# Deformable convolution, second layer: four gathered taps in even tiles, three in odd ones, and column positions loaded over the partitions instead of spread by matmuls

## The reference, cut to what matters

```python
def _L1_conv_ref(x, w_p, b_p, w_m, b_m, w_conv):
    offset = _conv2d(x, w_p, b_p, padding=1)                   # 18 maps: 9 rows, 9 columns
    m = jax.nn.sigmoid(_conv2d(x, w_m, b_m, padding=1))        # 9 weights
    p = offset + p_0[None] + p_n[None, :, None, None]          # place of every tap
    ...
    x_off = g_lt * gather(q_lt_x, q_lt_y) + g_rb * gather(q_rb_x, q_rb_y) \
          + g_lb * gather(q_lt_x, q_rb_y) + g_rt * gather(q_rb_x, q_lt_y)
    x_off = x_off * m                                          # 9 taps of 32 channels
    return _conv2d(x_off, w_conv, None, stride=KS, padding=0)
...
x = x + _L0_conv_ref(_gn(x), ...)
x = x + _L1_conv_ref(_gn(x), ...)
```

## Time and profile before

| | before |
|---|---|
| three timed runs | 558.33, 562.84, 563.54 us; median 562.84 |
| profiled execution, its own time | 557.18 us |
| span of that execution | 555.1 us |
| TensorE busy | 492.3 us, 89% of the span, 4214 matmuls |
| VectorE busy | 422.8 us, 76%, 941 instructions |
| ScalarE busy | 155.5 us, 28% |
| GpSimd busy | 261.6 us, 47% |
| DMA | 48.10 MB, mean 87 GB/s |

### The profile page before, as it was taken

One profiled execution on the slowest core, in us unless ns is written; L12 is line 12 of the kernel. 1 busy time (PEld: TensorE's weight loads), 2 busy tenths in 40 slices (PEclk: granted clock), 3 DMA queues, 4 the chain that ended last, 5 costly groups with the idle time before them and its releaser, 6 DMA issues.

```text
span 555.1 us, 11479 instructions
## 1 busy us (share of the span) xinstructions
PE 492.3 (89%) x4214; PEld 286.5 (52%) x4214; DVE 422.8 (76%) x941; ACT 155.5 (28%) x292; POOL 261.6 (47%) x272
## 2 busy tenths in 40 slices
PE   3687879988937799999999999999999999999994
PEld 3345445646626435454555555555545555465553
DVE  2455385779846498887978879888888888899892
ACT  3321120211035522323324233232232332332211
POOL 2177455547100177454544545555545454555520
PEclk9857798989986999999999999999999999999998
DMA  4899479577303871122121229111111111111100
GB/s 110 251 227 228 119 179 185 115 132 139 73 4 93 242 171 53 52 59 56 54 57 52 74 60 114 43 35 44 39 39 44 39 44 34 46 37 44 44 21 14
DMA packets 39879, 48.10 MB, mean 87 GB/s; under 512 B 15742, under 2 KB 31906, under 8 KB 39824
## 3 DMA queue, kind: packets, MB, share of 16 engines
q1 hardware_dynamic: 31464, 30.20, 24.9%
q0 software_dynamic: 8192, 16.79, 12.1%
q10 hardware_dynamic: 168, 0.34, 0.2%
HBM read 30.62 MB, written 8.72 MB: 71 GB/s over the span
## 4 chain that ended last, share of the span: by engine, by line
PE 73%; DVE 11%; DMA 5%; SPq 5%; issue 3%; ACT 2%; POOL 0%; DVEq 0%; ACTq 0%
PE ps_later L1166 12%; PE ps_pair L1166 10%; PE ps_raw L1147 8%; PE ps_x L1179 8%; PE ps_x L1183 5%; PE ps_x L1191 5%; PE ps_raw L976 5%; DVE vlast L1602 3%; PE ps_o L1207 3%; DMA xn<-xq 3%; PE ps_o L989 3%; SPq L475 2%; PE ps_pair L1041 2%; PE ps_x L1041 2%; DMA shared<-positions 2%
## 5 line engine op out<-in xcount | busy, mean ns | idle before, releaser
L611 POOL DMA_INDIRECT got<-table,idx x256 | 254.4, 994 | 218.2 <-DVE prod L1803 112.5
L1786 DVE TENSOR_TENSOR samples<-shared,vprod 128x800 f32<-128x800 f32 x48 | 47.1, 985 | 15.9 <-PE ps_x L1041 10.8
L1179 PEld LDWEIGHTS ps_x<-early,vprod 128*128 128x128 f32 x384 | 43.2, 144 | 30.5 <-issue 28.3
L1602 DVE TENSOR_TENSOR vprod<-ps_pair,rhat 128x704 f32<-128x704 f32 x64 | 56.6, 885 | 2.0 <-PE ps_pair L1166 1.7
L1602 DVE TENSOR_TENSOR vprod<-ps_later,rhat 128x704 f32<-128x704 f32 x64 | 56.6, 884 | 0.6 <-PE ps_later L1166 0.4
L1147 PE MATMUL ps_raw<-conv_out,later 128*128 128x512 f32 x96 | 53.9, 643 | 1.4 <-ACT shared L830 1.4
L1179 PE MATMUL ps_x<-early,vprod 128*128 128x128 f32 x384 | 54.8, 279 | 0.0
L1612 DVE TENSOR_TENSOR vprod<-vprod 128x640 f32<-128x640 f32 x64 | 52.4, 819 | 0.3
L1602 DVE TENSOR_TENSOR vlast<-ps_pair,rhat 128x704 f32<-128x704 f32 x32 | 28.5, 891 | 27.0 <-PE ps_pair L1166 26.7
L1166 PE MATMUL ps_later<-columns_of,shared 64*64 64x352 f32 x384 | 38.8, 474 | 4.2 <-DVE vlast L1602 3.7
L1166 PE MATMUL ps_later<-columns_of 64*64 64x352 f32 x384 | 38.9, 475 | 4.1 <-DVE vlast L1602 4.0
(11 more groups left out here) (215 smaller groups left out, 711.7 us busy)
## 6 DMA issues: line engine op xcount, KB each, us to landing
shared<-positions SPq DMA_DIRECT2D x24, 440.0 KB, 10.4
xn<-xq SPq DMA_DIRECT2D x52, 132.0 KB, 3.9
got<-table,idx POOLq DMA_INDIRECT x256, 8.0
table<-trow SPq DMA_DIRECT2D x9, 234.0 KB
table<-trow SPq DMA_DIRECT2D x2, 1024.0 KB, 5.1
out<-ysumT SPq DMA_DIRECT2D x64, 16.0 KB, 1.5
columns_of<-table SPq DMA_DIRECT2D x2, 512.0 KB, 9.4
table<-trow SPq DMA_DIRECT2D x1, 936.0 KB
```

What stands on the lines that cost most here:

```text
L611: pool.indirect_dma_start(into[t][:, s * P:(s + 1) * P], None, tab, bass.IndirectOffsetOnAxis(ap=idx[:, slot, k:k + 1], axis=0),).then_inc ...
L1179: nc.tensor.matmul(bank[:, P:2 * P], vprod[:, t % 2, r, :], idn[:], start=(r == 0), stop=(r == HALF - 1), is_transpose=True)
L1602: nc.vector.tensor_tensor(dst, ps_dense[pair_number(0, t, pair) % 2][:].rearrange("p (d n) -> p d n", d=2)[:, :, 0:WROWS * C].rearrange("p ...
L1786: nc.vector.tensor_tensor(wprod[t % 2].rearrange("p (y x c) -> p y x c", y=SIDE, c=C), window[n // TT % NWIN][:, :, 2 * t * C:(2 * t + SID ...
```

## The change

Even tiles now gather four taps and odd tiles three. An even tile so has five dense taps: two pairs, and tap 8 alone. Tap 8 of tiles 0 and 2 share one pair, made with tile 0, so a group has 11 pairs instead of 12, and tile 2 has only two. Tap 8 of both tiles goes into `vlast`, the third pair of odd tiles into a new `vtail`; three additions instead of four; an even tile turns two blocks of it instead of four. The gathers rise from 12 to 14 a group.

The spreads are left in place for groups 0 to 2 only (in two or three smaller matmuls, since even and odd tiles now take other taps). For groups 3 to 15 one matmul, `fold_parts`, folds the four parts of `conv_out` and picks out six rows of column positions (33 rows in `ps_raw`), and ScalarE copies them to `folded` with even tiles in the first half and odd ones in the second (`copy_folded`). SP writes the six rows to DRAM (`send_places`), and in a later group six DMAs read them back so that 64 partitions each hold the same row (`load_places`, 704 KB a group; the source steps by 0 over the partitions). ScalarE then takes the absolute value in place, with the partition's own column as a bias, where it took it from PSUM before. `turn_folded` transposes the 27 folded rows instead of `turn_parts`. The convolution moves from t = 2 to t = 1, the fold stands at t = 2 behind the outputs. `later` grows from 1,092 to 1,879 columns.

```diff
-GT = 3
-DT = 9 - GT
+GT_OF = (4, 3)
+GT = max(GT_OF)
+DENSE = min(GT_OF)
+DT = 9 - DENSE
-PAIRS = 3 * TT
+PAIRS = 3 * TT - 1
+SPREAD_GROUPS = 3
-LATER = dict(fold_proj=P, conv_w1=4 * 32, grid1=27, grid2=27, w4=9 * C, steps1=WROWS, spread=SPREADS * P, wd0=C, wd=C, wlast=C,
+LATER = dict(fold_proj=P, conv_w1=4 * 32, grid1=TT * 27, rows1=NG * TT * GT, grid2=27, w4=9 * C, steps1=WROWS, spread=2 * SPREADS * P, wd0=C, wd4=C, wd3=C, wlast=C, fold1=27 + DT, away=1,
...
         def pairs_of(t):
-            return range(3)
+            return range(2 if t == 2 else 3)
...
+            def send_places(n):
+                sp.wait_ge(fold_sb, n - SPREAD_GROUPS + 1)
+                if n >= SPREAD_GROUPS + 2:
+                    sp.wait_ge(chat_come, 96 * (n - 1 - SPREAD_GROUPS))
+                sp.dma_start(places_of[n % 2], folded[27:27 + DT, :]).then_inc(places_out, 16)
+            def load_places(n):
+                sp.wait_ge(places_out, 16 * (n - SPREAD_GROUPS + 1))
+                sp.wait_ge(v_mm, 4 * PAIRS * (n - 1))
+                half, at = GPIX // 2, n % 2 * DT * GPIX
+                for h in range(2):
+                    to = chat[n % 2][W * h:W * (h + 1)]
+                    sp.dma_start(to[:, 0:2, 0:half], bass.AP(places_of.tensor, at + (1 + h) * GPIX, [
+                        [0, W], [2 * GPIX, 2], [1, half]])).then_inc(chat_come, 16)
+                    sp.dma_start(to[:, :, half:GPIX], bass.AP(places_of.tensor, at + h * GPIX + half, [
+                        [0, W], [2 * GPIX, SPREADS], [1, half]])).then_inc(chat_come, 16)
+                    sp.dma_start(to[:, 2, 0:P], bass.AP(places_of.tensor, at + (DT - 1) * GPIX + h * P, [
+                        [0, W], [1, P]])).then_inc(chat_come, 16)
...
+            for g in range(NG):
+                if SPREAD_GROUPS <= g + 1 < NG:
+                    load_places(g + 1)
+                for c in ROWS_IN.get(g, []):
                     sp.wait_ge(tab_copied, NT + PT + c + 1)
                     send_rows(table[1][1], range(c, c + 1), tab_out["11"])
...
+                if g + 3 < NG:
+                    send_places(g + 3)
+                if g:
+                    store((g - 1) // GB, (g - 1) % GB, (g - 1) % 2)
+                if PT - 1 in ROWS_IN.get(g, []):
+                    load_columns(1)
...
             def column_weights(g, u, k):
-                act.wait_ge(spread_mm, SPREADS * g + k + 1)
-                nc.scalar.activation(chat[u][:, k, :], ps_raw[:, :], ACT.Abs).then_inc(chat_abs, 1)
+                if isinstance(g, int) and g < SPREAD_GROUPS:
+                    act.wait_ge(spread_mm, SPREADS * g + k + 1)
+                    nc.scalar.activation(chat[u][:, k, :], ps_raw[:, :], ACT.Abs).then_inc(chat_abs, 1)
+                else:
+                    if k == 0:
+                        act.wait_ge(chat_come, 96 * (g - SPREAD_GROUPS + 1))
+                    nc.scalar.activation(chat[u][:, k, :], chat[u][:, k, :], ACT.Abs,
+                                         bias=away[:, 0:1]).then_inc(chat_abs, 1)
...
+            def fold_parts(n):
+                pe.wait_ge(conv_sb, NG + n + 1)
+                nc.tensor.matmul(ps_raw[0:27 + DT, :], fold1[:, :], conv_out[n % 2][:], start=True,
+                                 stop=True).then_inc(fold_mm, 1)
+            def turn_folded(n):
+                pe.wait_ge(fold_sb, n - SPREAD_GROUPS + 1)
+                pe.wait_ge(conv_read, NI + n)
+                for t in range(TT):
+                    last = nc.tensor.transpose(ps_conv[1][:, t, :], folded[0:27, slot_of(t):slot_of(t) + P], idn[0:27, 0:27])
+                last.then_inc(conv_mm, 1)
...
                     elif t == 2:
                         fill(2, 4)
+                        if conv:
+                            fold_parts(g + 3)
                         if rows[1:]:
-                            pe.wait_ge(chat_abs, SPREADS * (g + 2))
+                            pe.wait_ge(fold_sb, g + 1)
                             make_rows(1, rows[1:], NT + PT, tab_copied, tab_mm, [ps_raw])
...
-                    gather(table[1][b], GT, u, t, arrived[1][t])
+                    gather(table[1][b], GT_OF[t % 2], u, t, arrived[1][t], stride=GT)
...
-                dve.wait_ge(v_read, pairs_done(g, t))
-                nc.vector.tensor_tensor(vlast[:, t % 2, 0:WROWS - KEPT, :], vlast[:, t % 2, 0:WROWS - KEPT, :],
-                                        vlast[:, t % 2, KEPT:WROWS, :], ALU.add).then_inc(v_added, 1)
+                if t != 2:
+                    dve.wait_ge(v_read, pairs_done(g, t))
+                    low, high = ((vlast[1][:, 0:WROWS - KEPT, :], vlast[1][:, KEPT:WROWS, :]) if t % 2 else
+                                 (vlast[0][:, :, 0:WROWS - KEPT, :], vlast[0][:, :, KEPT:WROWS, :]))
+                    nc.vector.tensor_tensor(low, low, high, ALU.add).then_inc(v_added, 1)
```

More of the change, by code:

```diff
@@ L1146, in spread_columns @@
                     pe.wait_ge(v_mm, 4 * PAIRS * (g - 1))
-                last = nc.tensor.matmul(ps_raw[:, :], spr[:, k, :], conv_out[g % 2][:], start=True, stop=True)
-                last.then_inc(spread_mm, 1)
+                half = GPIX // 2
+                columns_in_tiles = conv_out[g % 2][:].rearrange("p (a t n) -> p a t n", t=2, n=P)
+                if k < 2:
+                    nc.tensor.matmul(ps_raw[:, 0:half], spr[:, 0, k, :], columns_in_tiles[:, :, 0, :], start=True, stop=True)
+                else:
+                    for h in range(2):
+                        nc.tensor.matmul(ps_raw[W * h:W * (h + 1), 0:P], spr[:, 0, k, W * h:W * (h + 1)],
+                                         columns_in_tiles[:, h, 0, :], start=True, stop=True)
+                last = nc.tensor.matmul(ps_raw[:, half:GPIX], spr[:, 1, k, :], columns_in_tiles[:, :, 1, :], start=True,
+                                        stop=True)
+                last.then_inc(spread_mm, 1)
+            def fold_parts(n):
[8 more added lines that the diff above has]
+                last.then_inc(conv_mm, 1)
             def interpolate(tile, pair):
@@ L1180, in turn_samples @@
                                      stop=(r == HALF - 1), is_transpose=True)
-                pe.wait_ge(v_added, 2 * tile + 2)
-                for a in range(0, KEPT, 2):
-                    last = nc.tensor.matmul(bank[:, 2 * P:3 * P],
-                                            vlast[:, t % 2, a:a + 2, :].rearrange("p w c -> p (w c)"), idn[:],
-                                            start=(a == 0), stop=(a + 2 == KEPT), is_transpose=True)
+                pe.wait_ge(v_added, additions_done(tile // TT, t))
+                kept, n = (vlast[1], 2) if t % 2 else (vlast[0][:, t // 2], CORNERS)
+                for a in range(0, KEPT, n):
+                    last = nc.tensor.matmul(bank[:, 2 * P:3 * P], kept[:, a:a + n, :].rearrange("p w c -> p (w c)"), idn[:],
+                                            start=(a == 0), stop=(a + n == KEPT), is_transpose=True)
                 last.then_inc(v_turned, 1)
-                if tile == 0:
+                if tile == 1:
                     pe.wait_ge(prod_clear, 1)
@@ L1262, in _ @@
                         interpolate(tile + 1, pair)
-                    if t == 0 and g + 1 < NG:
-                        if g + 2 < NG:
-                            pe.wait_ge(conv_sb, NG + g + 3)
+                    if t == 0 and spread:
+                        pe.wait_ge(conv_sb, NG + g + 3)
                         if rows:
```

187 lines of the change are left out of this document (120 added, 67 removed).

## The result

The changed kernel takes 534.4 us (median of four runs, 531.7 to 539.1) against 560.6 (558.3 to 563.5) in the same comparison: ratio 0.954, interval 0.945 to 0.963. Two later comparisons gave 0.960 (0.954 to 0.966) and 0.957 (0.951 to 0.964). Medians here are over all runs of a kernel, ratios only over its fast ones, those within 1.5% of its fastest.

What follows compares the result with a forecast made beforehand. TensorE's issue, coupled to VectorE by two pairs of banks, was taken to bound layer 2. Gains of 22.2 less 5.3, 2 and 1.6 gave 13.3, so 557.18 became 543.9 profiled, 550 by the median; range 538 to 565.

Steps and rivals of the forecast that it cites:

- What bounds it: Layer 2: a group costs what TensorE issues; VectorE waits, only 2 us apart, and two pairs of banks couple them.
- A steady group: Groups 6 to 12 of layer 2: period from 21.72 to 20.3, a gain of 1.45 each, 10.2 in all.
- The late load: Group 7's places queue behind the second image's columns on SP: TensorE waits 5.3 at group 6's fold, plus 2 of clock.
- The places: SP's six loads a group, 704 KB: landing taken as 7 (bounds 3.3 and 9.9), hidden up to 9.7.
- the rival of late places: Landing beyond 9.7 delays eleven groups by one per microsecond; chance 0.17 at the edge, 0.13 later than that.
- The rule of half rate: Copies whose partitions step through HBM together by 4 MiB run at 103 GB/s; for the places, about 9 with issue.
- The constants: Before layer 2: the larger `later`, 403 KB more on SP, delays the second image's shifts by 1.6 (bounds 0 and twice that).
- the sum: Whole kernel: 22.2 - 5.3 - 2 - 1.6 = 13.3 less, from 557.18 to 543.9 in the profile.
- The tail: Last groups of layer 2: group 13 gains 2, group 14 gains 3, group 15 gains 1.
- Groups 0 and 1: First groups of layer 2 keep spreads: a pair saved against a wait of about a copy, zero.
- The range: Whole kernel, 8 in 10: low end 538 (no late load, transposes 0.3 cheaper), high end 565 (landing 11.1 in eleven groups).
- The engines overlap better: Rival: tile 3's new wait vanishes, period 18.8, 16 less, 533 by the median; chance 0.10, shared with no late load.

Runs made afterwards that it cites:

- turn_thrice: Changed kernel with each group's turn of the 27 folded rows done three times over; 541.3 us, ratio to the kernel before 0.975.
- taps_alone: Changed kernel's gathers, pairs and spreads in halves, with the kernel before's TensorE order, ScalarE group and SP loop, no fold or transfers; 540.5 us, ratio 0.971.
- fold_behind: Changed kernel with the fold behind tile 3's third pair (groups with at most one table row) and ScalarE's copy later; 527.9 us, ratio to before 0.949.
- changed_again: The changed kernel, unchanged, run again as common measure in a later comparison; 537.8 us, ratio to before 0.960.

## Why the prediction was right or wrong

**What bounds it** was right: TensorE and VectorE coupled by the two pairs of banks, GpSimd and the queues under them. The list of waits of the steady group came true in kind, with 0.82 for 0.94 at the new place.

**A steady group** was to be 20.3 and was 19.9. The step that failed is the turn of the folded rows, left at zero because "no row shows transposes of 27 rows". It takes 0.36, where the row that it replaces takes 1.00, and brings the pair behind it 0.53 earlier, so the prediction's own bound (0.57 cheaper) was the right value, and turn_thrice shows that such a sum reaches the period in full. With it went the wait of 0.5 at tile 0's third product, which was to stay. It is 0.5 a group; in every second one 0.34 of it is lost again to the pause, which the prediction did not have. In groups 2 to 5, to which turn_thrice added 0.5 as well, it is also why they gained 2.0 each and not 1.5.

**The late load** was right in its place, its mechanism and nearly its size: 4.85 of wait and 1.5 of clock for 5.3 and 2, 5.6 to 6.3 by its removal. The places landed 14.3 after SP came to the columns (323.89 to 338.15), for a forecast L of 15. The columns are two loads of 512 KB each, and the prediction's estimate by the Trainium skill counted 512 KB once. The Trainium skill (DMA: Bandwidth & Descriptors, Anatomy of one DMA) gives its 2.0 us and 436 GB/s for DMAs that GpSimd issues; an estimate by it is 4.4 us for both, and the wait would have fallen away. That did not hold for these loads, which SP issued in pieces of 128 bytes; the row of 11.4 us did.

**The places** landed in 7.5 for an assumed 7, under a threshold of 9.0 to 9.4 for 9.7; the rival of late places was priced by bytes, and up to twice the bytes it was SP's issuing that counted, 4.1 for six loads where I had 2.4. The rule of half rate that the prediction weighed (the Trainium skill, DMA: Bandwidth & Descriptors, Latency and other measured facts) would by an estimate have wanted 14 us for the 1.4 MB of the doubled loads, which landed in 11.0 to 12.0 with their issue.

**The constants** failed as a term: +1.6 was forecast, and the stretch came out 2.7 earlier. A price shows in the kernel before (1.4 at that convolution for one load, 3.6 for four), but the stretch ended between 194.4 and 203.8 in 14 traces, so neither -2.7 nor +1.6 could have been read from one pair of profiles. Of the 12 us between the sum and the profile 4.3 are this.

**The tail** was to give 6. Up to ScalarE's last activation it gave 6.8 (62.44 to 55.61), half of it, 3.3, by the taps (59.11 in taps_alone). The other 2.6 of its 9.4 are the unexplained end.

**Groups 0 and 1** lost 1.0 instead of nothing; taps_alone has them 1.0 faster than before, so it is what came with the fold that costs, and 1.2 of it go when the fold moves behind the third pair (42.9 in fold_behind, 44.1 in changed_again).

Together: the turn with the pause 0.4 x 7 and 0.5 x 4, in sum 4.8; start 4.3; tail 0.8 and end 2.6; late load 1.0; groups 0 and 1 -1.0. That makes 12.5 for a miss of 12.1. **The range** failed because its low end took in 0.3 a group for cheaper transposes and the late load, but no scatter of the start and nothing at the end. **"The engines overlap better"**, 18.8 a group, was not what happened: VectorE's new wait stayed, and fold_behind, which takes it away, reached 19.3.

## What to carry to other kernels

When two engines are coupled, write down between which two of the slower engine's releases each moved piece of work falls: here the 0.50 added to the turn passed into the period in full although both engines had waits, and moving one matmul gave back 0.6 a group. An operation that no row shows is better taken at its cheap bound and its dear one in two sums than at no change. A new load goes ahead of anything large that is not needed sooner in the same queue, and its landing is to be counted from the last issue. Set stages, not whole spans, against each other: layer 2 repeated to 0.7 of 335, while the stretch ahead of it moved by 9 in 14 traces.

## What the hardware showed

- Four transposes of 27 rows take 0.36; the four matmuls to 27 columns that they replace are eight records in the trace and take 1.00. The pair behind the same fourteen blocks starts 2.04 after the turn instead of 2.57. Eight more transposes added 0.50.
- Loads that repeat one row over 64 partitions landed 2.9 to 4.3 after the end of their last issue, whether six or twelve were issued, and 11.0 to 12.0 after the first for 1.4 MB.
- Between the layers the granted clock fell to the lower level in some executions and not in others of the same program, behind a stretch at 0.50 from 165 to 170 and one at 1.00 from 180 to 185 in both; it is worth 4.7 us.
